# Down projection of the channel mix in split fp16, between the shared expert's products, and one write of zeros behind the experts' ends

## Chip, core and metric

The kernel runs on one core of a Trainium2 chip. The metric is the device time of one launch in microseconds (us). The engines are TensorE (PE, its weight loads PEld), VectorE (DVE), ScalarE (ACT), GpSimd (POOL) and SyncE (SP), which only issues DMAs. Each runs its own instruction queue in order; semaphores join them.

## Reference

`x` is 4096 tokens of 256 channels. With `LN` a layer norm without scale:

```
x = x + LN(rwkv(LN(x)))          # a time mix, then a channel mix
x = x + LN(moe(LN(x)))           # a shared expert and one of 8 routed experts per token
```

The channel mix in `rwkv`, on the result x2 of the time mix (`shift` moves by one token, ln2 with scale and offset):

```
xn2 = ln2(x2);  xk2, xr2 = two mixes of xn2 and shift(xn2)
kf  = square(relu(xk2 @ Wk_ffn.T))         # 1024 wide
kv  = kf @ Wv_ffn.T                        # the down projection, 1024 -> 256
x3  = x2 + sigmoid(xr2 @ Wr_ffn.T) * kv
```

The time mix is a recurrence over tokens (running maximum, numerator, denominator). Each expert is `gelu(x @ W1) * (x @ W2) @ W3`, width 1024; the routed one is the argmax of `x @ Wg`.

## The kernel before

**Stages.** The 4096 tokens are 16 chunks (NC) of 256 tokens. A software pipeline walks over steps i = -1 to 17 (`chunk_steps`; the middle steps run in a hardware loop, two steps to a turn). In step i the time mix works on chunk c0 = i, the channel mix on c1 = i-1, the shared expert and the choice of the routed expert on c2 = i-2, the end of the shared expert and the scatter of the tokens into rows by expert on c3 = i-3. Behind the steps come 39 slots of 128 rows for the routed experts (`slot_steps`).

**Split operands.** Most products run in fp16 with each operand split in a high and a low half: hi = fp16(v), by ScalarE, and lo = fp16(v - hi), by GpSimd or VectorE. `three` (L378 to L382) issues hi*hi, hi*lo and lo*hi into one sum. Weights are split once: `pieces` lists them, SP loads a piece (`load_own`), ScalarE writes its high half (`own_hi`), VectorE its low half (`own_lo`); OWN_LOADS, OWN_HI and OWN_LO say in which step. The down projection (L586, L589), the output projection of the time mix (L602) and the transposes (L389) are fp32. Its weights `w_fv` come by one DMA.

**Down projection.** For the four quarters q of 1024 hidden channels: TensorE `channel_mix_up(q)` into an `up` bank; ScalarE `relu_up(q)` (L796) into `relu_k[q % 2]` and `square(q)` (L804) into `kf`; TensorE `channel_mix_down(q)` takes the quarter's two tiles for the first 128 tokens, and with q = 3 all eight tiles for the other 128.

**Order of the queues.** Written out by hand, one list per engine and step. The names that the rest uses:

- TensorE: projection(0), (1), transposes of normed2 (`transpose_normed2`, L389), ranks, projection(2), `shared_down` of c3, transposes of xf, gate, `shared_gate`/`shared_up` 0 and 1, receptance, `channel_mix_up(0)`, `(1)`, transposes of the next chunk (`transpose_next`, L389), `channel_mix_up(2)`, `(3)`, then as in the code printed below.
- ScalarE: `xnT_norm` (L709) writes the next chunk's normalized, transposed input xnT from these transposes; `mix_hi(m)` (L831) the high halves of the mixes; `ln2` (L715) normed2.
- VectorE: `halo` (L1039, the column of xnT before its first token), `den_r` (L1116), `num` (L1131), `mix0` (L1049, the mixes for k, v and r from xnT and delta), `divide` (L1121), `rw` (L1136), mix0 for r, `x3_gate`, `x3_sum`, `x2_sum`, moments.
- GpSimd: delta2, inverse(0) (ten small operations for a norm), `now`, delta (L1549, xnT minus its shift), `mix_lo(0)`, `mix_lo(1)` (L1602), `sh_lo(0)` (L1596), scatter of c3 (two indirect DMAs, L1637), `sh_lo(1)`, `mix_lo(2)`, inverse(2), an offset (L1541), inverse(1) (its last operation is L1518), which `ln2` needs, `sh_lo(2)`, inverse(3), `sh_lo(3)`.

**Zeros.** The tokens of an expert end anywhere in a slot; the rows behind them must hold zeros. In step 16 (NC), ahead of the stores of the last split expert weights, SP writes zeros and a mark behind the tokens so far, 5 x 128 rows per expert, columns ID and up (`zeros_behind_tokens`, L304); GpSimd's scatter of the last chunks waits for these. In step 17 it writes 128 rows of the lower columns at each expert's end (`zeros_at_ends`, L313), then issues the first slots' loads (`first_slots`).

## Time and profile before

| | |
|---|---|
| three runs | 1004.53, 1005.79, 1005.34 us, median 1005.34 |
| profiled execution | 1005.74 us, its span 1004.0 us |
| busy TensorE, VectorE, ScalarE, GpSimd | 928.7, 722.7, 585.7, 587.6 us |
| DMA over the span | 156 GB/s |
| chunk steps, then slots | to about 670 us, then to 1004 us |

Times in the rows are microseconds from the start of the span. Busy time is the union of an engine's instructions, without the time in which its queue waits; a matmul's row shows its way through the pipeline, so starts, not ends, tell the pace of TensorE. "PEclk" is the clock granted to TensorE as a share of 2.4 GHz. What stands in brackets behind an instruction is how long its engine idled before it, and what released it.

### The profile page before, as it was taken

The page shows a single profiled execution, that of the slowest core. Times are in us where ns is not written, and L with a number is a line of the kernel's source. Part 1 is how long each engine was busy: PE and PEld are TensorE (multiplying, and loading weights), DVE is VectorE, ACT ScalarE, POOL GpSimd, SP SyncE. Part 2 cuts the span into 40 slices and gives each one's busy share as a digit, 9 for nine tenths or more (in the row PEclk, how much of TensorE's full clock was granted, in tenths as well). Part 3 has the DMA queues.
Part 4 walks back from the last instruction along what each step waited for, and adds up shares of the span by engine and source line. Part 5 has one row for each costly group of instructions (what it writes and reads, how often), then busy time and mean ns, then how long its engine had stood idle before and what let it go on. Part 6 is the DMA issues. An engine that isn't in the chain of part 4 may idle for free.

```text
span 1004.0 us, 28041 instructions
## 1 busy us (share of the span) xinstructions
PE 928.7 (93%) x9734; PEld 838.7 (84%) x9734; DVE 722.7 (72%) x1653; ACT 585.7 (58%) x1014; POOL 587.6 (59%) x800
## 2 busy tenths in 40 slices
PE   3377999999999999999999999699999999999994
PEld 2266888888888888888888888589999999999994
DVE  6888999999999999999999984444444444444442
ACT  4485778877878878868868855233333333333330
POOL 5446567667767867866866540454555555555553
PEclk9697999999999999999999999799999999999998
DMA  7212242351351252252152259845787788576510
GB/s 239 65 54 68 90 178 63 120 191 50 120 212 50 96 209 67 80 209 98 48 210 95 86 191 317 283 171 172 253 271 235 236 261 270 163 256 207 167 57 22
DMA packets 87339, 156.37 MB, mean 156 GB/s; under 512 B 5549, under 2 KB 68142, under 8 KB 82160
## 3 DMA queue, kind: packets, MB, share of 16 engines
q1 hardware_dynamic: 40352, 78.25, 22.9%
q10 hardware_dynamic: 42368, 60.38, 18.7%
q0 software_dynamic: 4560, 16.98, 4.4%
q8 instruction: 34, 0.56, 0.2%
q14 instruction: 25, 0.20, 0.1%
HBM read 183.59 MB, written 50.51 MB: 233 GB/s over the span
## 4 chain that ended last, share of the span: by engine, by line
PE 65%; DVE 9%; issue 9%; POOL 7%; ACTq 4%; ACT 3%; DMA 1%; POOLq 0%; DVEq 0%
PE up L380 13%; PE up L382 12%; PE up L381 12%; PE yp L380 6%; PE yp L382 6%; PE yp L381 6%; PE yp L586 2%; PE yp L589 2%; PE yp L602 2%; ACTq L933 2%; PE tp L389 2%; DVE arena L1020 1%; POOL mix_s L1602 1%; DVE er L1121 1%; POOL routed_rows L1637 1%
## 5 line engine op out<-in xcount | busy, mean ns | idle before, releaser
L380 PE MATMUL up<-mix_s,arena 128*128 128x128 f16 x1248 | 211.1, 219 | 0.4 <-DVE ex L1468 0.3
L381 PE MATMUL up<-mix_s,arena 128*128 128x128 f16 x1248 | 211.0, 219 | 0.0
L382 PE MATMUL up<-mix_s,arena 128*128 128x128 f16 x1248 | 211.0, 219 | 0.0
L380 PE MATMUL up<-xf_s,arena 128*128 128x256 f16 x512 | 140.7, 275 | 1.9 <-issue 1.9
L381 PE MATMUL up<-xf_s,arena 128*128 128x256 f16 x512 | 140.8, 275 | 0.0
L382 PE MATMUL up<-xf_s,arena 128*128 128x256 f16 x512 | 140.7, 275 | 0.0
L1700 POOL TENSOR_TENSOR kf_s<-ex,kf_s 128x512 f16<-128x512 f32 x78 | 90.2, 1156 | 84.1 <-ACT kf_s L979 84.0
L1468 DVE SCALAR_TENSOR_TENSOR ex<-up,ex 128x512 f32<-128x512 f32 x78 | 53.9, 692 | 102.1 <-ACT ex L973 101.9
L380 PEld LDWEIGHTS up<-mix_s,arena 128*128 128x128 f16 x1248 | 122.1, 98 | 1.3 <-DVE ex L1468 1.1
L381 PEld LDWEIGHTS up<-mix_s,arena 128*128 128x128 f16 x1248 | 122.1, 98 | 0.4
L382 PEld LDWEIGHTS up<-mix_s,arena 128*128 128x128 f16 x1248 | 122.1, 98 | 0.0
L973 ACT ACTIVATE ex<-up 128x512 f32<-128x512 f32 x78 | 45.9, 589 | 106.3 <-issue 57.2
L1596 POOL TENSOR_TENSOR sh_s<-gu,sh_s 128x512 f16<-128x512 f32 x64 | 76.1, 1190 | 43.0 <-ACT sh_s L824 42.7
L979 ACT ACTIVATE kf_s<-ex 128x512 f16<-128x512 f32 x78 | 49.1, 630 | 79.0 <-DVE ex L1468 67.3
L380 PE MATMUL yp<-arena,kf_s 128*128 128x256 f16 x312 | 85.0, 273 | 0.7 <-issue 0.7
L382 PE MATMUL yp<-arena,kf_s 128*128 128x256 f16 x312 | 85.0, 273 | 0.0
L381 PE MATMUL yp<-arena,kf_s 128*128 128x256 f16 x312 | 85.0, 273 | 0.0
L380 PE MATMUL yp<-arena,sh_s 128*128 128x256 f16 x256 | 71.2, 278 | 12.4 <-POOL sh_s L1596 12.4
L1602 POOL TENSOR_TENSOR mix_s<-mixed,mix_s 128x512 f16<-128x512 f32 x48 | 57.9, 1221 | 42.3 <-ACT mix_s L831 42.3
L381 PE MATMUL yp<-arena,sh_s 128*128 128x256 f16 x256 | 71.2, 278 | 0.0
L382 PE MATMUL yp<-arena,sh_s 128*128 128x256 f16 x256 | 71.1, 278 | 0.0
L380 PE MATMUL up<-mix_s,w_fk 128*128 128x256 f16 x256 | 70.1, 274 | 0.0
(228 smaller groups left out, 2864.8 us busy)
## 6 DMA issues: line engine op xcount, KB each, us to landing
arena<-w_split ACTq DMA_DIRECT2D x113, 1024.0 KB
arena<-in_W SPq DMA_DIRECT2D x24, 1024.0 KB, 6.6
w_split<-arena SPq DMA_DIRECT2D x24, 1024.0 KB, 9.3
rows<-routed_rows ACTq DMA_DIRECT2D x39, 261.0 KB, 3.0
arena<-w_split SPq DMA_DIRECT2D x9, 1024.0 KB
routed_rows<-x_in SPq DMA_DIRECT2D x8, 650.0 KB, 6.3
normed<-routed_rows ACTq DMA_DIRECT2D x37, 128.0 KB, 2.4
x_in<-in_x SPq DMA_DIRECT2D x16, 256.0 KB, 2.8
```

The costliest lines, as they stand in the source:

```text
L380: pe.matmul(out, stat(0), mov(0), start=first, stop=False)
L381: pe.matmul(out, stat(0), mov(1), start=False, stop=False)
L382: return pe.matmul(out, stat(1), mov(0), start=False, stop=last)
L389: m = pe.transpose(bank[:, k, t * P:(t + 1) * P], src[:, t, k * P:(k + 1) * P], ident[:])
L586: pe.matmul(yp[1][:, 0, :], kf[:, f, 0:P], w_fv[:, f, :], start=(f == 0), stop=(f == FT - 1))
L589: m = pe.matmul(yp[1][:, 1, :], kf[:, f, P:CH], w_fv[:, f, :], start=(f == 0), stop=(f == FT - 1))
L973: act.activation(slot_g[q], up[2 * q][:].rearrange("p k n -> p (k n)"), ACT.Gelu, scale=1 / WS).then_inc(S("slot_gelu"), 1)
L979: act.activation(slot_h[b][:, 0, q * FT // 2:(q + 1) * FT // 2, :], slot_g[q].rearrange("p (f n) -> p f n", n=P), ACT.Copy).then_inc(S("sl ...
L1468: dve.scalar_tensor_tensor(out=slot_g[q], in0=up[2 * q + 1][:].rearrange("p k n -> p (k n)"), scalar=HS / WS, in1=slot_g[q], op0=ALU.mult, ...
L1596: pool.tensor_tensor(sh_s[:, 1, 2 * g:2 * g + 2, :], gu[g % GUS][:], sh_s[:, 0, 2 * g:2 * g + 2, :], ALU.subtract).then_inc(S("sh_lo"), 1)
L1602: pool.tensor_tensor(mix_s[m][:, 1], mixed[m][:], mix_s[m][:, 0], ALU.subtract).then_inc(S("mix_lo"), 1)
L1700: pool.tensor_tensor(hs[:, 1], slot_g[q].rearrange("p (f n) -> p f n", n=P), hs[:, 0], ALU.subtract).then_inc(S("slot_h_lo"), 1)
```

## The change

- `w_fv` becomes a split piece (number 7, in buffer 2), loaded and split like the others. `kf` is kept as split halves in `kf_s`: `square(q)` stays in `relu_k`, ScalarE copies the high half (`kf_hi`), GpSimd subtracts for the low half (`kf_lo`), and `channel_mix_down` uses `three` in place of the fp32 product. The factor WS moves out of `x3_sum`.
- TensorE's order behind `channel_mix_up(3)`: `shared_gate(2)`, down 0 and 1, `shared_up(2)`, down 2 and 3, `output`.
- ScalarE's and GpSimd's lists get the new operations; `delta_of` stands between `kf_lo(1)` and `kf_lo(2)`.
- The zeros behind the tokens go. Zeros are written once, in step 17, whole rows, 128 at each expert's end, and the first slots wait for them; the scatter and the slots' later loads no longer do.
- In step 16 `sh_lo(1)` goes ahead of the scatter; in step 17 VectorE's `shared(2)` goes ahead of `last_slots`.

```diff
--- before.py
+++ after.py
@@ -67,7 +67,7 @@
         w_fk = sb("w_fk", [2, CT, F], F16)
-        w_fv = sb("w_fv", [FT, C])
+        w_fv = sb("w_fv", [2, FT, C], F16)
         w_gate = sb("w_gate", [2, CT, E], F16)
@@ -120,11 +120,9 @@
         relu_k = [sb(f"relu_k{b}", chan) for b in range(2)]
-        zero_row = x_in.rearrange("p t d -> p (t d)")[:, 0:ROW - ID]
-        zero_rest = ex.rearrange("p n k c -> p (n k c)")[:, 2 * CT * CH:2 * CT * CH + ID]
+        zero_row = ex.rearrange("p n k c -> p (n k c)")[:, 2 * CT * CH:2 * CT * CH + ROW]
         mixed2 = relu_k
         kf_s = sb("kf_s", [2, FT, CH], F16)
-        kf = kf_s.rearrange("p h f n -> p (h f n)").bitcast(F32).rearrange("p (f n) -> p f n", f=FT)
         sh_s = sb("sh_s", [2, FT, CH], F16)
@@ -150,7 +148,6 @@
         expert_int = sb("expert_int", [2, E], I32)
-        zero_at = sb("zero_at", [E], I32)
         end_at = sb("end_at", [E], I32)
@@ -192,14 +189,16 @@
             pieces.append((tiles(a[n]), (CT, CT, FT)[m], (F, F, C)[m], shared_w[:, m]))
+        pieces.insert(7, (tiles(a["fvT"]), FT, C, flat(w_fv)))
         N_OWN = len(pieces)
-        NEEDS_KVR, NEEDS_FFN, NEEDS_SHARED = 3, 6, 8
-        OWN_HI = {(-2, 0): (0, 3), (-1, 2): (3, 4), (0, 0): (4, 6), (0, 2): (6, 7), (1, 1): (7, 9)}
-        OWN_LO = {(-2, 0): (0, 3), (-1, 1): (3, 4), (0, 1): (4, 6), (1, 3): (6, 7), (2, 3): (7, 8), (2, 0): (8, 9)}
-        OWN_LOADS = {(-1, 0): (4, 6), (0, 0): (6, 7), (0, 1): (8, 9), (1, 1): (7, 8)}
-        OWN_BUFFER = [0, 1, 2, 4, 0, 1, 3, 1, 4]
+        NEEDS_KVR, NEEDS_FFN, NEEDS_FV, NEEDS_SHARED = 3, 6, 8, 9
+        OWN_HI = {(-2, 0): (0, 3), (-1, 2): (3, 4), (0, 0): (4, 6), (0, 2): (6, 8), (1, 1): (8, 10)}
+        OWN_LO = {(-2, 0): (0, 3), (-1, 1): (3, 4), (0, 1): (4, 6), (1, 3): (6, 7), (1, 0): (7, 8), (2, 3): (8, 9),
+                  (2, 0): (9, 10)}
+        OWN_LOADS = {(-1, 0): (4, 6), (0, 0): (6, 8), (0, 1): (9, 10), (1, 1): (8, 9)}
+        OWN_BUFFER = [0, 1, 2, 4, 0, 1, 3, 2, 1, 4]
         own_raw = raw + [c.rearrange("p h n -> p (h n)").bitcast(F32) for c in cut]
@@ -292,25 +291,14 @@
             load_own(3)
-            sp.dma_start(w_fv[:], tiles(a["fvT"])).then_inc(S("fv_in"), 16)
-            def zeros_behind_tokens():
-                sp.wait_ge(S("zero_at"), 1)
+            def zeros_at_ends():
+                sp.wait_ge(S("end_at"), 1)
                 sp.wait_ge(S("zero_row"), 1)
-                n = 2 * CH // P + 1
-                for e in range(E):
-                    at = sp.value_load(zero_at[0:1, e:e + 1], min_val=0, max_val=E * REGION - n * P)
-                    sp.dma_start(routed_rows[bass.ds(at, n * P), ID:].rearrange("(n p) d -> p n d", p=P),
-                                 zero_row.unsqueeze(1).broadcast_to([P, n, ROW - ID])).then_inc(S("zeroed"), 16)
-            def zeros_at_ends():
-                sp.wait_ge(S("end_at"), 1)
-                sp.wait_ge(S("zero_rest"), 1)
                 for e in range(E):
                     at = sp.value_load(end_at[0:1, e:e + 1], min_val=0, max_val=E * REGION - P)
-                    sp.dma_start(routed_rows[bass.ds(at, P), 0:ID], zero_rest).then_inc(S("zeroed_rest"), 16)
+                    sp.dma_start(routed_rows[bass.ds(at, P)], zero_row).then_inc(S("zeroed"), 16)
@@ -337,6 +325,7 @@
                 sp.wait_ge(S("scattered_xf"), 16 * TT)
+                sp.wait_ge(S("zeroed"), 16 * E)
                 for b in range(2):
@@ -360,8 +349,6 @@
                     load_expert(e, m)
-                if at_step(i, NC):
-                    zeros_behind_tokens()
                 for e, m in early_piece(i, p, h) + last_late(i, p, h) + late_now(i, p, h):
@@ -371,8 +358,6 @@
-            sp.wait_ge(S("zeroed"), 16 * E)
-            sp.wait_ge(S("zeroed_rest"), 16 * E)
@@ -578,16 +563,17 @@
                     if at_step(i, 1) and q == 0:
-                        pe.wait_ge(S("fv_in"), 16)
+                        pe.wait_ge(S("piece_lo"), NEEDS_FV)
                     if q == 0:
                         wait(pe, S("y_sh"), c1 - 1)
-                    wait(pe, S("kf"), 4 * c1 + q + 1)
+                    wait(pe, S("kf_lo"), 4 * c1 + q + 1)
                     for f in (2 * q, 2 * q + 1):
-                        pe.matmul(yp[1][:, 0, :], kf[:, f, 0:P], w_fv[:, f, :], start=(f == 0), stop=(f == FT - 1))
+                        three(pe, yp[1][:, 0, :], lambda s: kf_s[:, s, f, 0:P], lambda s: w_fv[:, s, f, :],
+                              f == 0, f == FT - 1)
                     if q == 3:
                         for f in range(FT):
-                            m = pe.matmul(yp[1][:, 1, :], kf[:, f, P:CH], w_fv[:, f, :], start=(f == 0),
-                                          stop=(f == FT - 1))
+                            m = three(pe, yp[1][:, 1, :], lambda s: kf_s[:, s, f, P:CH], lambda s: w_fv[:, s, f, :],
+                                      f == 0, f == FT - 1)
                         m.then_inc(S("fv_mm"), 1)
@@ -654,11 +640,13 @@
                     ranks(c2)
-                for q in range(4):
-                    channel_mix_down(q)
                 shared_gate(2)
+                channel_mix_down(0)
+                channel_mix_down(1)
+                shared_up(2)
+                channel_mix_down(2)
+                channel_mix_down(3)
                 output()
-                shared_up(2)
                 shared_gate(3)
@@ -792,7 +780,7 @@
                         wait(act, S("fk_mm"), n + 1)
-                        wait(act, S("kf"), n - 1)
+                        wait(act, S("kf_lo"), n - 1)
                         act.activation(relu_k[q % 2][:], up[(11 + q) % 4][:], ACT.Relu,
@@ -800,8 +788,14 @@
                         wait(act, S("relu"), n + 1)
+                        act.activation(relu_k[q % 2][:], relu_k[q % 2][:], ACT.Square).then_inc(S("kf"), 1)
+                def kf_hi(q):
+                    if on(c1):
+                        wait(act, S("kf"), 4 * c1 + q + 1)
                         wait(act, S("fv_mm"), c1)
-                        act.activation(kf[:, 2 * q:2 * q + 2, :], relu_k[q % 2][:], ACT.Square).then_inc(S("kf"), 1)
+                        act.activation(kf_s[:, 0, 2 * q:2 * q + 2, :], relu_k[q % 2][:],
+                                       ACT.Copy).then_inc(S("kf_hi"), 1)
@@ -891,12 +885,16 @@
                 relu_up(1)
+                kf_hi(0)
+                square(1)
                 xnT_norm()
-                square(1)
+                kf_hi(1)
                 relu_up(2)
+                square(2)
+                kf_hi(2)
                 relu_up(3)
-                square(2)
                 square(3)
+                kf_hi(3)
                 sigmoid()
@@ -981,7 +979,6 @@
                         act.wait_ge(S("scattered_rest"), 16 * TT * 2)
-                        act.wait_ge(S("zeroed_rest"), 16 * E)
                     at = rows_of(j)
@@ -1053,7 +1050,7 @@
                 wait(dve, S("delta2"), c + 1)
-                wait(dve, S("kf"), 4 * c)
+                wait(dve, S("kf_lo"), 4 * c)
                 for m in (1, 0):
@@ -1156,7 +1153,7 @@
                 wait(dve, S("x3a"), c + 1)
-                dve.scalar_tensor_tensor(out=gate_r[:], in0=gate_r[:], scalar=0.5 * WS, in1=x2[:],
+                dve.scalar_tensor_tensor(out=gate_r[:], in0=gate_r[:], scalar=0.5, in1=x2[:],
                                          op0=ALU.mult, op1=ALU.add).then_inc(S("x3"), 1)
@@ -1278,8 +1275,6 @@
                     placing(c3, 1 - p, h + p - 2)
-                if at_step(i, NC):
-                    zeros_after()
                 if on(c1):
@@ -1299,6 +1294,7 @@
                     places_of_slots()
+                    shared(2)
                     last_slots()
@@ -1348,7 +1344,8 @@
                     x2_moments(c0)
-                shared(2)
+                if not at_step(i, NC + 1):
+                    shared(2)
                 if at_step(i, NC):
@@ -1364,15 +1361,8 @@
                     dve.wait_ge(S("denominator"), 4 * NC)
-                    dve.memset(zero_rest, 0.0).then_inc(S("zero_rest"), 1)
+                    dve.memset(zero_row, 0.0).then_inc(S("zero_row"), 1)
                 own(2)
-            def zeros_after():
-                dve.wait_ge(S("normed"), TT * NC)
-                dve.memset(zero_row, 0.0).then_inc(S("zero_row"), 1)
-                dve.wait_ge(S("next_row"), NC - 2)
-                dve.tensor_copy(zero_at[:], next_row[:, 0, :]).then_inc(S("zero_at"), 1)
@@ -1596,6 +1586,12 @@
+                def kf_lo(q):
+                    if on(c1):
+                        wait(pool, S("kf_hi"), 4 * c1 + q + 1)
+                        pool.tensor_tensor(kf_s[:, 1, 2 * q:2 * q + 2, :], relu_k[q % 2][:],
+                                           kf_s[:, 0, 2 * q:2 * q + 2, :], ALU.subtract).then_inc(S("kf_lo"), 1)
@@ -1627,8 +1623,6 @@
                     if on(c) and not at_step(i, NC + 1):
-                        if at_step(c, NC - 2):
-                            pool.wait_ge(S("zeroed"), 16 * E)
                         wait(pool, S("placed"), c + 1)
@@ -1655,13 +1649,20 @@
                 now_of()
+                kf_lo(0)
+                kf_lo(1)
                 delta_of()
+                kf_lo(2)
+                kf_lo(3)
                 scatter_expert_input()
...
                 sh_lo(0)
+                if at_step(i, NC):
+                    sh_lo(1)
                 scatter(c3, 1 - p)
-                sh_lo(1)
+                if not at_step(i, NC):
+                    sh_lo(1)
                 mix_lo(2)
```

## Rows read from the trace of the kernel before

**Rows 1.** Stretch, us, busy (x) of PE, PEld, DVE, ACT, POOL; PEclk, DMA, GB/s
```profile
110.00:600.00 490.00, 487.41 (x4111) 431.55 (x4109) 456.51 (x1017) 384.64 (x659) 339.33 (x447) 1.00 0.34 121
```

**Rows 2.** Groups by line and shape: count, busy us, mean ns, idle before
```profile
L979 ACT ACTIVATE kf_s<-ex 128x512 f16<-128x512 f32 x78 | 49.1, 630 | 79.0 <-DVE ex L1468 67.3 <-PE yp L382 10.4 <-PE up L382 1.4
...
L1014 DVE SCALAR_TENSOR_TENSOR w_fk<-arena,w_fk 128x2048 f16<-128x2048 f32 x1 | 2.3, 2284 | 0.0
...
L1700 POOL TENSOR_TENSOR kf_s<-ex,kf_s 128x512 f16<-128x512 f32 x78 | 90.2, 1156 | 84.1 <-ACT kf_s L979 84.0
```

**Rows 3.** Timeline of TensorE: start us, us, instruction, [idle before it <- releaser]
```profile
121.44 0.60 PE L389 MATMUL tp<-ident,normed 128*128 128x128 f32 x4
...
306.19 0.65 PE L389 MATMUL tp<-ident,normed 128*128 128x128 f32 x4 [0.17 <-ACT normed L715]
...
323.32 0.60 PE L389 MATMUL tp<-ident,normed 128*128 128x128 f32 x4
...
326.37 3.62 PE L586 MATMUL yp<-w_fv,kf_s 128*128 128x256 f32 x16
...
333.28 0.27 PE L380 MATMUL up<-xf_s,arena 128*128 128x256 f16 x1
...
334.59 1.89 PE L602 MATMUL yp<-w_o,val 128*128 128x256 f32 x8
...
342.87 0.60 PE L389 MATMUL tp<-ident,normed 128*128 128x128 f32 x4
...
600.53 0.66 PE L389 MATMUL tp<-ident,normed 128*128 128x128 f32 x4 [1.08 <-ACT normed L715]
```

**Rows 4.** Timeline of ScalarE in the step from 306 to 343 us
```profile
323.26 0.63 ACT L804 ACTIVATE kf_s<-relu_k 128x512 f32<-128x512 f32 x1
...
324.25 1.04 ACT L709 ACTIVATE xnT<-tp,vec 128x256 f32<-128x256 f32 x2
...
341.68 1.07 ACT L715 ACTIVATE normed<-x,inv 128x256 f32<-128x256 f32 x2
```

**Rows 5.** Timeline of GpSimd in the same step
```profile
309.28 1.04 POOL L1549 TENSOR_TENSOR delta<-xn2T 128x512 f32<-128x512 f32 x1 [0.90 <-DVE xn2T L1039]
...
325.65 1.43 POOL L1549 TENSOR_TENSOR delta<-xnT 128x512 f32<-128x512 f32 x1 [4.37 <-DVE xnT L1039]
329.29 2.28 POOL L1602 TENSOR_TENSOR mix_s<-mixed,mix_s 128x512 f16<-128x512 f32 x2 [2.21 <-ACT mix_s L831]
...
341.32 0.20 POOL L1518 TENSOR_TENSOR inv<-inv 128x2 f32<-128x2 f32 x1
```

**Rows 6.** Timeline of VectorE in the same step
```profile
325.32 0.17 DVE L1039 COPY xnT<-xnT 128x2 f32<-128x2 f32 x1 [0.67 <-ACT xnT L709]
...
326.10 1.53 DVE L1131 TENSOR_TENSOR val<-mixed,dist 128x512 f32<-128x512 f32 x1
327.55 1.66 DVE L1049 SCALAR_TENSOR_TENSOR mixed<-delta,vec,xnT 128x256 f32<-128x256 f32 x4
...
332.51 0.72 DVE L1136 TENSOR_TENSOR val<-val,er 128x512 f32<-128x512 f32 x1
```

**Rows 7.** Timelines of VectorE and GpSimd in the next step
```profile
363.39 0.16 DVE L1039 COPY xnT<-xnT 128x2 f32<-128x2 f32 x1
...
367.13 2.27 POOL L1602 TENSOR_TENSOR mix_s<-mixed,mix_s 128x512 f16<-128x512 f32 x2 [2.08 <-ACT mix_s L831]
```

**Rows 8.** Busy time in one stretch behind the middle, columns as in rows 1
```profile
600.00:610.00 10.00, 8.38 (x76) 7.00 (x77) 8.15 (x17) 6.03 (x11) 4.01 (x7) 0.83 0.86 287
```

**Rows 9.** Timelines of SP's queue, GpSimd and TensorE behind the last chunk
```profile
604.39 12.96 SPq L304 DMA_DIRECT2D routed_rows<-x_in  x8
...
641.84 0.20 POOL L1541 TENSOR_TENSOR rows<-mv,inv 128x2 f32<-128x2 f32 x1 [5.75 <-DMA routed_rows<-rows,row_of]
...
643.39 0.40 PE L380 MATMUL yp<-arena,sh_s 128*128 128x256 f16 x1 [7.36 <-POOL sh_s L1596]
...
654.08 9.26 SPq L313 DMA_DIRECT2D routed_rows<-ex  x8
```

More of the change, by code:

```diff
@@ L294, in _ @@
             load_own(3)
-            sp.dma_start(w_fv[:], tiles(a["fvT"])).then_inc(S("fv_in"), 16)
-            def zeros_behind_tokens():
-                sp.wait_ge(S("zero_at"), 1)
-                sp.wait_ge(S("zero_row"), 1)
-                n = 2 * CH // P + 1
-                for e in range(E):
-                    at = sp.value_load(zero_at[0:1, e:e + 1], min_val=0, max_val=E * REGION - n * P)
-                    sp.dma_start(routed_rows[bass.ds(at, n * P), ID:].rearrange("(n p) d -> p n d", p=P),
-                                 zero_row.unsqueeze(1).broadcast_to([P, n, ROW - ID])).then_inc(S("zeroed"), 16)
             def zeros_at_ends():
                 sp.wait_ge(S("end_at"), 1)
-                sp.wait_ge(S("zero_rest"), 1)
+                sp.wait_ge(S("zero_row"), 1)
                 for e in range(E):
                     at = sp.value_load(end_at[0:1, e:e + 1], min_val=0, max_val=E * REGION - P)
-                    sp.dma_start(routed_rows[bass.ds(at, P), 0:ID], zero_rest).then_inc(S("zeroed_rest"), 16)
+                    sp.dma_start(routed_rows[bass.ds(at, P)], zero_row).then_inc(S("zeroed"), 16)
             def half(w, part):
```

## Prediction

> **What bounds the kernel now.** I read the busy time of the long middle stretch first, then the timeline of each engine over one chunk step, then the stretch behind the last chunk. In the middle TensorE is busy 487.4 of 490 us at a granted clock of 1.00 [rows 1]. That looks like a kernel bound by TensorE alone, in which every microsecond of products taken away comes back. The timelines correct this. The transposes of normed2 mark a step: thirteen steps between the first and the last of these rows take (600.53 - 121.44)/13 = 36.85 us each [rows 3]. ScalarE's normalization that these transposes need runs from 341.68 to 342.75, and they start at 342.87 [rows 3, 4]: they start the moment it lands. In the step before, TensorE idled 0.17 us there for the same instruction [rows 3]. So there is a second limit of the same length as TensorE's work. Follow it back: the normalization waits for GpSimd's inverse(1), which ends at 341.52; GpSimd has worked in an unbroken row up to it since mix_lo(0) at 329.29, 12.2 us earlier [rows 5]; mix_lo(0) comes behind VectorE's mix0, at 327.55, which waited for GpSimd's delta (325.65 to 327.08), and that for the halo column at 325.32 [rows 5, 6]. The halo comes from the transposes at 323.32. Between 306.19 and 323.32 TensorE works without a gap, on nothing that the change touches [rows 3]. This is a ring: transposes of normed2, 17.1 us of products, transposes of the next chunk, GpSimd's queue, transposes of normed2. The down projection (326.37 to 333.28) lies beside the ring.
>
> **TensorE's saving.** The 32 products of the down projection, fp32 now, take 333.28 - 326.37 = 6.91 us by 16 products (two records each). A split product of the same 256 columns costs (334.59 - 333.28)/12 = 0.109 us [rows 3], so 16 x 3 of them take 5.24 us. That is 1.67 us a step less, 27 us over 16 chunks, if TensorE's work set the time. That a split product is dearer than this is excluded by the same row.
>
> **ScalarE.** Four copies kf_hi per chunk, 0.63 us each [rows 2], 0.5 us apart where they don't wait for the instruction before them (square(0) at 323.26, one other, then the normalization at 324.25 [rows 4]). kf_hi(0) takes the place of the normalization of xnT, and with square(1) ahead of it too that moves 1.0 us, to 325.25 to 326.3. kf_hi(1) ends at 326.9. relu(2), square(2), kf_hi(2), relu(3), square(3), kf_hi(3) each wait for the one before, in good part: kf_hi(2) ends near 328.75 and kf_hi(3) near 330.6. ScalarE has room for these.
>
> **GpSimd.** Four subtractions kf_lo, 1.156 us each by the row of the same form [rows 2], 4.6 us a step, in the middle of the ring. It idled 4.37 us before delta [rows 5], and kf_lo(0), from 325.0 to 326.15, hides there. kf_lo(1) can't start before 326.95, and delta now stands behind it; kf_lo(2) and kf_lo(3) stand between delta and mix_lo(0). What is queued behind these is everything down to inverse(1), so the whole unbroken row of 12.2 us moves with mix_lo(0).
>
> How much? The halo is at 326.35. VectorE and GpSimd get in each other's way on operations that read two operands from SBUF: delta took 1.43 us while VectorE worked on such operations and 1.04 in another place of the step [rows 5], and VectorE's num took 1.53 us beside it while the equally large rw took 0.72 [rows 6]. I take that over. kf_lo(1) is held until about 327.15 by den_r and ends at 328.3; num waits for that and ends at 328.85; delta goes to 329.75; kf_lo(2), which has been ready, goes first and ends at 330.9, while VectorE's four mix0 (1.66 us [rows 6]) wait. Then these and kf_lo(3) share 2.55 us, in either order (if kf_lo(3) is first, mix_hi(0) is late; if mix0 is first, kf_lo(3) is), so mix_lo(0) starts at 333.45 and not at 329.29: +4.15 us. In every other step VectorE reaches the halo late by its own queue (363.39, mix_lo(0) at 367.13 [rows 7]), later than the moved xnT: there kf_lo(1) ends at 365.15, delta at 366.6, kf_lo(2) at 367.8, mix_lo(0) starts at 370.35: +3.2 us. The mean is 3.7 us a step.
>
> The lower bound leaves out the blocking: 1.04 for delta, kf_lo(3) right behind kf_hi(3), mix_lo(0) at 331.75 and 368.3, which is +2.4 and +1.2, mean 1.8. I take 3.7, since both rows show the blocking at just this place.
>
> The Trainium skill, "SBUF - State Buffer", section on who interferes with whom, says that a VectorE instruction with two SBUF inputs and a GpSimd instruction that reads SBUF exclude each other for a whole instruction. By that rule the step grows 3.7 us, without it 1.8; the trace agrees (1.53 us against 0.72).
>
> **On TensorE beside the ring.** down(2) waits until 331.0 for kf_lo(2), down(3) until some 333.5 for kf_lo(3), output then for rw, whose reciprocal starts 3 us later than before. The output ends near 339 instead of 336.3; gate(3), up(3) and two projections (5.24 us) bring TensorE to 344.3, and the normed2 transposes come at 342.87 + 4.15 = 347.0. So TensorE idles 2 to 3 us there and some 2.5 us earlier, 5.5 us a step, and the 1.67 us saved is part of that idle time. The moved shared_up(2) covers the wait for down(2), and can't cover more.
>
> **The ring's steps.** There are 15 intervals between transposes of normed2 with a down projection in them (the 13 above and the two before 121.44). 15 x 3.7 = 55 us.
>
> **The clock.** Between 600 and 610 us two idle stretches of about 1.1 us (the first is in [rows 3]) are followed by a mean granted clock of 0.83 [rows 8]: 10 x (1 - 0.83) = 1.7 us of work lost at 1.2 GHz instead of 2.4. Whether 2 to 3 us of idle before the transposes do that in each step is open: between nothing and 15 x 1.7 = 26 us. I take one step in four, 7 us.
>
> **The beginning.** The down weights become a split piece: one more VectorE pass of 2.28 us [rows 2] in a step where VectorE is busy, and one on ScalarE: between 0 and 4 us, I take 2.
>
> **The end.** The zeros behind the tokens occupy SP's queue for 12.96 us ahead of the last stores [rows 9]; without them the last expert piece, x3_gate and with it the scatter come 2 to 3 us earlier, and so does the landing for which GpSimd waited 5.75 us and TensorE then 7.36 us [rows 9]. The landing itself stays. shared(2) ahead of last_slots gives up to 1 us. Against that, the zeros at the ends (9.26 us of SP queue from 654.08 [rows 9]) are rows 1.5 times as long and must now have landed before the first slots are read: between 0 and 4 us, I take 1.5. Together -2, between -8 and +3.
>
> **Sum** against the profiled execution's own 1005.74 us (span 1004.0): + 55 + 7 + 2 - 2 = 1067.7. The median is 0.4 us lower: 1067.
>
> **Rivals.** Less than 0.2% (2 us) can't be told from no change here.
> 1. The ring grows as above, with the clock falling in a few steps: 1050 to 1080 us. Chance 0.50.
> 2. The blocking between VectorE and GpSimd is lighter: 15 x 1.8 = 27 us and the small terms, 1033; with half of it 1047. For it: which engine wins is not shown by a row. 1025 to 1050: 0.23.
> 3. The clock falls in every step: 1005.3 + 55 + 26 = 1086. For it: TensorE now idles 5.5 us a step. Against it: the row shows it behind two stretches in close succession only [rows 8]. Above 1080: 0.15.
> 4. Faster. The tight fit of normalization and transposes is a result of TensorE's pace and GpSimd's idle 4.37 us in front of delta takes up the four subtractions: then 27 us go, with the end 29, to 976. It decides if mix_lo(0) starts no later after the transposes of the next chunk than the 5.97 us of now (329.29 - 323.32). Against it: kf_lo(1) can't start before 326.95. Chance 0.08.
> 5. Both effects meet near nothing (a shift of some 0 to 1 us): 0.04.
>
> The range that leaves out no more than 2 in 10 reaches from 1033 (rival 2's bound) to 1090. Faster 0.08, same 0.03, slower 0.89.
>
> **What the changed kernel's profile would show.** The transposes of normed2 about 40.5 us apart, with idle time on TensorE in front of them put down to ScalarE's normalization; TensorE's busy share in the middle near 87%; GpSimd's delta some 3 us later behind the transposes of the next chunk and mix_lo(0) 9 to 10 us behind them instead of 6 to 7; num and mix0 stretched; down(2) and down(3) waiting for GpSimd. If mix_lo(0) is late but the transposes are not, the ring is drawn wrong; if they are 35 us apart, rival 4 holds; half clock behind each idle stretch is rival 3.

## The result and the profile after

Slower: 1052.31 us median (1049.34 to 1054.52, 4 runs) against 1004.98 us (4 runs), a ratio of 1.0469, 95% interval 1.0453 to 1.0485. The profiled execution took 1049.34 us, its span 1047.5 us: 43.5 us more than the span of before. Of all runs told here one was slow and is left out, 5311 us for the kernel before with fewer products and the scatters early.

Where the 43.5 us are is read from the marks of the steps. First the timeline of TensorE in the kernel after; the transposes of normed2 (L374; those at 344.40 are of the next chunk) answer to [rows 3]:

```profile
126.13 0.38 PE L374 MATMUL tp<-ident,normed 128*128 128x128 f32 x2
...
344.40 0.60 PE L374 MATMUL tp<-ident,normed 128*128 128x128 f32 x4
...
353.23 0.28 PE L365 MATMUL yp<-w_fv,kf_s 128*128 128x256 f16 x1 [0.46 <-POOL kf_s L1592]
...
358.33 0.48 PE L588 MATMUL yp<-w_o,val 128*128 128x256 f32 x1 [1.65 <-DVE val L1133]
...
366.98 0.33 PE L374 MATMUL tp<-ident,normed 128*128 128x128 f32 x1 [0.16 <-ACT normed L703]
...
643.16 0.44 PE L374 MATMUL tp<-ident,normed 128*128 128x128 f32 x2 [2.28 <-ACT normed L703]
```

Thirteen steps take (643.16 - 126.13)/13 = 39.77 us each, 2.92 more than before. From the first transposes of normed2 (48.88 us here, 49.79 before) to the last, the 15 steps take 594.28 us against 550.74: all 43.5 us. What lies ahead is 0.9 us shorter, what lies behind 0.9 longer. From the transposes of the next chunk to those of normed2 the step shown takes 22.58 us against 19.55, the following one (384.10 to 407.16) 23.06 against 20.04 (359.94 to 379.98): +3.0 each. The other part, 344.40 - 327.27 = 17.13 us, is what it was.

The middle stretch in the kernel after (windows, columns as in [rows 1]), and its longest waits (engine, line, released by: us in total, times, longest):

```profile
110.00:640.00 530.00, 475.64 (x4321) 411.59 (x4322) 490.83 (x1011) 420.04 (x712) 399.20 (x496) 1.00 0.32 111
```

```profile
PE yp L588 <- DVE val L1133: 22.3, 13, 2.6
PE yp L365 <- POOL kf_s L1592: 15.0, 27, 1.3
PE up L365 <- DVE gu L1241: 14.2, 13, 1.2
...
PE tp L374 <- ACT normed L703: 2.9, 9, 1.2
```

TensorE is 90% busy at a granted clock of 1.00, not 99%. Its idle time, 54 us or 4.1 us a step, lies ahead of the output projection, the down projection and the first projection, not ahead of the transposes.

VectorE, GpSimd and ScalarE in the step of 344.40 (timelines of the kernel after), to be held against [rows 4 to 6]:

```profile
347.44 0.17 DVE L1036 COPY xnT<-xnT 128x2 f32<-128x2 f32 x1 [1.71 <-ACT xnT L697]
...
348.22 1.65 DVE L1128 TENSOR_TENSOR val<-mixed,dist 128x512 f32<-128x512 f32 x1
350.88 3.37 DVE L1046 SCALAR_TENSOR_TENSOR mixed<-delta,vec,xnT 128x256 f32<-128x256 f32 x4 [1.01 <-POOL delta L1539]
354.17 3.34 DVE L1118 RECIPROCAL er<-er 128x512 f32<-128x512 f32 x1
357.55 0.73 DVE L1133 TENSOR_TENSOR val<-val,er 128x512 f32<-128x512 f32 x1
...
360.61 0.48 DVE L1140 SCALAR_TENSOR_TENSOR x<-normed,spread,yp 128x256 f32<-128x256 f32 x1
...
363.20 0.15 DVE L1026 BATCH_NORM_AGGREGATE mv<-stats 128x2 f32<-128x6 f32 x1
```

```profile
348.00 1.32 POOL L1592 TENSOR_TENSOR kf_s<-relu_k,kf_s 128x512 f16<-128x512 f32 x1 [0.79 <-ACT kf_s L797]
349.28 1.49 POOL L1539 TENSOR_TENSOR delta<-xnT 128x512 f32<-128x512 f32 x1
350.73 2.44 POOL L1592 TENSOR_TENSOR kf_s<-relu_k,kf_s 128x512 f16<-128x512 f32 x2
354.20 1.15 POOL L1598 TENSOR_TENSOR mix_s<-mixed,mix_s 128x512 f16<-128x512 f32 x1 [1.02 <-ACT mix_s L825]
...
364.04 0.44 POOL L1498 TENSOR_TENSOR inv<-mv,eps_ws 128x2 f32<-128x2 f32 x1
...
365.61 0.20 POOL L1508 TENSOR_TENSOR inv<-inv 128x2 f32<-128x2 f32 x1
```

```profile
346.37 1.03 ACT L697 ACTIVATE xnT<-tp,vec 128x256 f32<-128x256 f32 x2
```

Counted from the transposes of the next chunk (t0): xnT starts at t0 + 1.97 (before 0.93), the halo at 3.04 (before 2.00), mix0 at 6.48 (before 4.23), mix_lo(0) at 9.80 (before 5.97), rw at 13.15 (before 9.19), x2_sum at 16.21 (before 13.20), the end of inverse(1) at 21.41 (before 18.20). So the four mix0 take 3.37 us beside GpSimd's subtractions instead of 1.66 [rows 6], and VectorE's row has moved by 1.0 us at the halo and by 3.0 at x2_sum, about as GpSimd's has at inverse(1) (3.2).

Which row ends last can be read where they meet. GpSimd works from mix_lo(0) to inverse(1) without a wait for another engine. The moments of x2 are ready at 363.35, 0.7 us before inverse(1) begins (364.04); in the step of 384.10 it is the same 0.7. The moments of x3 are ready 0.3 us before inverse(2), in both. So GpSimd's row ends last, and VectorE's is only 0.3 us shorter.

### The profile page after: what moved, and what is told of

It reads as the page before. It is cut to its first block, busy times and chain, and to the rows that moved or that the text cites. A ratio compares the mean times of both kernels' runs of the same rounds, so it can differ in the third digit from the quotient of the medians.

```text
span 1047.5 us, 28645 instructions
## 1 busy us (share of the span) xinstructions
PE 911.9 (87%) x9990; PEld 813.7 (78%) x9990; DVE 763.0 (73%) x1652; ACT 629.1 (60%) x1079; POOL 661.9 (63%) x864
## 4 chain that ended last, share of the span: by engine, by line
PE 27%; DVE 17%; issue 16%; POOL 15%; ACTq 13%; ACT 6%; DMA 3%; SPq 1%; POOLq 0%; DVEq 0%
ACTq L931 6%; PE up L365 5%; PE up L367 5%; PE up L366 5%; PE yp L365 3%; PE yp L366 3%; PE yp L367 3%; ACTq L954 3%; DVE mixed L1046 2%; POOL kf_s L1592 2%; DVE er L1118 2%; ACTq L934 2%; POOL mix_s L1598 2%; POOL routed_rows L1631 2%; DMA routed_rows<-rows,row_of 2%
## 5 line engine op out<-in xcount | busy, mean ns | idle before, releaser
L1592 POOL TENSOR_TENSOR kf_s<-relu_k,kf_s 128x512 f16<-128x512 f32 x64 | 83.6, 1314 | 95.7 <-ACT kf_s L797 95.7
L365 PE MATMUL yp<-w_fv,kf_s 128*128 128x256 f16 x256 | 70.9, 277 | 18.8 <-POOL kf_s L1592 18.8
L365 PE MATMUL yp<-arena,sh_s 128*128 128x256 f16 x256 | 71.2, 278 | 12.5 <-POOL sh_s L1586 12.5
L1046 DVE SCALAR_TENSOR_TENSOR mixed<-delta,vec,xnT 128x256 f32<-128x256 f32 x96 | 65.8, 737 | 9.3 <-POOL delta L1539 9.3
```

The source lines that it names most:

```text
L365: pe.matmul(out, stat(0), mov(0), start=first, stop=False)
L1046: dve.scalar_tensor_tensor(out=mixed[m][:, k, :], in0=delta[:, k, :], scalar=vec[:, MK + m, k:k + 1], in1=x[:, k, 0:CH], op0=ALU.mult, op1 ...
L1592: pool.tensor_tensor(kf_s[:, 1, 2 * q:2 * q + 2, :], relu_k[q % 2][:], kf_s[:, 0, 2 * q:2 * q + 2, :], ALU.subtract).then_inc(S("kf_lo"), 1)
```

## The experiments

"The kernel before" and "the kernel after" are the two of the change; each edit is to one of them.

**Is TensorE's saving worth anything?** The kernel before with fewer products, and with only the edits of the zeros and of the end.

```diff
-                        for f in range(FT):
+                        for f in range(FT // 2):
```

> The kernel before, with 4 of the 8 fp32 products of the down projection's second 128 tokens left out: 4 x 0.43 = 1.73 us less for TensorE a chunk, as much as the change saves it, and nothing else touched. Ring theory (the queue of GpSimd sets the step, TensorE only keeps pace): 1003 to 1005 us, the transposes of normed2 still 36.8 us apart, idle time of 1.7 us a step on TensorE in front of them. Rival (TensorE sets the time): 16 x 1.73 = 28 us less, 977.

Measured 1004.11 us against 1005.12, ratio 0.9992 (0.9981 to 1.0003), a step of 36.84 us against 36.91. 1.73 us a step less on TensorE are worth nothing. Rival 4 fell here: something of the same length as TensorE's work holds the step. In this trace it is GpSimd's row: 12.29 us from mix_lo(0) to inverse(1) in the step of t0 = 324.40, without a wait for another engine; meanwhile the moments of x3 on VectorE are ready 1.1 us before inverse(2) begins.

> The kernel before, with the change's zeros alone: one write behind the ends, no zeros behind the tokens, sh_lo(1) ahead of the scatter in step 16, shared(2) ahead of the last slot table in step 17. As predicted for the end: 2 to 4 us less, 1002. Rival (the first slots wait for the landing of the zeros, the scatter's landing is as late as before): 0 to 2 us more, 1006.

Measured 1005.36 us, ratio 1.001 (0.9998 to 1.0021): the rewritten zeros, the moved sh_lo(1) and shared(2) are worth nothing either way. The 2 to 4 us that I expected did not come.

**Which part costs what?** The kernel after with the low halves' subtraction cut to 8 columns of one tile (first diff), then the high halves' copy too (second), what is no longer written being zeroed once at the start; and the kernel before with the new order of TensorE alone, still with fp32 products.

```diff
-    pool.tensor_tensor(kf_s[:, 1, 2 * q:2 * q + 2, :], relu_k[q % 2][:],
-                       kf_s[:, 0, 2 * q:2 * q + 2, :], ALU.subtract)
+    pool.tensor_tensor(kf_s[:, 1, 2 * q:2 * q + 1, 0:8], relu_k[q % 2][:, 0:1, 0:8],
+                       kf_s[:, 0, 2 * q:2 * q + 1, 0:8], ALU.subtract)
```

> The changed kernel, with GpSimd's kf_lo cut to 8 columns of one tile (the low half stays zero elsewhere); waits, ScalarE's copies and the split products all stay. Ring theory: the four subtractions on GpSimd and their blocking are the whole loss; what stays is xnT one microsecond late in every other step: 36.8 to 37.4 us a step, 1005 to 1014 us. Rival (the dependent copies on ScalarE, or TensorE's waits for the halves, cost it): most of the 47 us stay, 1035 or more.

```diff
-    act.activation(kf_s[:, 0, 2 * q:2 * q + 2, :], relu_k[q % 2][:], ACT.Copy)
+    act.activation(kf_s[:, 0, 2 * q:2 * q + 1, 0:8], relu_k[q % 2][:, 0:1, 0:8], ACT.Copy)
```

> The changed kernel with both kf_lo on GpSimd and kf_hi on ScalarE cut to 8 columns of one tile (the halves stay zero elsewhere). TensorE's new order and its 1.67 us fewer a step stay, with next to no cost on the other engines. Theory as mended by e2 and e3 (the serial copies on ScalarE and the subtractions on GpSimd are the cost; the order costs only where the down projection ends late): the ring is as before, and TensorE's saving is worth nothing: 1003 to 1012 us. Rival 1 (the order alone costs 31 us in the changed kernel too): 1030 or more. Rival 2 (TensorE's saving shows once the halves are free): 980.

```diff
-    for q in range(4):
-        channel_mix_down(q)
     shared_gate(2)
+    channel_mix_down(0)
+    channel_mix_down(1)
+    shared_up(2)
+    channel_mix_down(2)
+    channel_mix_down(3)
     output()
-    shared_up(2)
```

> The kernel before, fp32 products as they were, with TensorE's order of the change alone (shared_gate(2), down 0 and 1, shared_up(2), down 2 and 3, output). Output comes 1.31 us later, and its way over x2 to GpSimd's inverse(1) had 0.55 us to spare: 0.7 us a step, 15 steps, 1010 to 1018 us. Rival (the order is free since the products are the same): 1005.

Measured: 1035.19 us without most of the subtraction (1.0306, 1.0284 to 1.0328), 1009.75 us without most of either (1.0047, 1.0029 to 1.0065), 1036.61 us for the order alone (1.0318, 1.0296 to 1.034). The first and the last missed what I expected.

With both halves cut, 4.5 us of the 47 are left. Giving ScalarE its full copies back costs 25.4 us more, giving GpSimd its subtractions 17.1 more, in this order; the subtractions without the copies were not run. I had priced ScalarE's copies at nothing but the moved xnT. VectorE and ScalarE in the step of t0 = 334.40, the kernel after with the small low halves:

```profile
337.44 0.17 DVE L1036 COPY xnT<-xnT 128x2 f32<-128x2 f32 x1 [1.70 <-ACT xnT L697]
...
339.92 1.67 DVE L1046 SCALAR_TENSOR_TENSOR mixed<-delta,vec,xnT 128x256 f32<-128x256 f32 x4 [1.01 <-POOL delta L1539]
...
344.89 1.66 DVE L1133 TENSOR_TENSOR val<-val,er 128x512 f32<-128x512 f32 x1
```

```profile
340.92 0.63 ACT L797 ACTIVATE kf_s<-relu_k 128x512 f16<-128x512 f32 x1
341.45 0.58 ACT L805 ACTIVATE gate_r<-yp 128x512 f32<-128x512 f32 x1
341.93 0.62 ACT L825 ACTIVATE mix_s<-mixed 128x512 f16<-128x512 f32 x1
```

The mixes take 1.67 us again, so it is GpSimd's subtractions that stretch them to 3.37. But the halo is still 3.04 us behind the transposes, and mix_hi(0) (L825), queued behind the last copy and the sigmoid, starts only at t0 + 7.5. GpSimd's mix_lo(0) then comes at t0 + 8.2 in both kinds of steps (before 5.97 and 7.19: 1.6 us later in the mean, and the step is 38.67 us, 1.8 longer), and its row runs on past the reciprocal: rw takes 1.66 us and not 0.73. So GpSimd's 4.6 us of subtractions are not the cause alone.

The order alone costs 31 us because the fp32 down projection, now behind gate(2) and up(2), ends later. VectorE and GpSimd in that kernel:

```profile
348.90 0.69 DVE L1156 SCALAR_TENSOR_TENSOR gate_r<-gate_r,yp 128x512 f32<-128x512 f32 x1 [2.09 <-PE yp L589]
...
351.55 0.87 DVE L1145 SCALAR_TENSOR_TENSOR x<-normed,spread,yp 128x256 f32<-128x256 f32 x2
```

```profile
353.45 0.20 POOL L1510 TENSOR_TENSOR inv<-mv,eps_ws 128x2 f32<-128x2 f32 x1 [2.60 <-DVE mv L1031]
```

x3_gate waits 2.09 us for the down projection, x3_sum behind it takes 1.78 us beside GpSimd instead of 0.69, x2_sum stands behind both in VectorE's queue, and GpSimd's inverses wait 2.60 us for VectorE. A second way to the same end: through VectorE, not through GpSimd's row.

**Is TensorE's old order better with split operands?** The kernel after with the order of before.

> The changed kernel with TensorE's old order (down 0 to 3, shared_gate(2), output, shared_up(2)). If the order costs here what it costs in e3: 31 us less, 1021. By the traces, the down projection now ends when kf_lo(3) has come, whatever the order, and TensorE waits for rw afterwards: 1040 to 1052 us.

Measured 1057.41 us (1.0522, 1.0503 to 1.054), 5 us worse than the change and above both cases that I had named. The products wait for the low halves anyway (45.3 us in the stretch from 110 to 640 us, 15.0 with the new order, whose gate(2) and up(2) fill that wait), so the 31 us that the order costs on fp32 products aren't there to be saved. The two costs don't add.

What the 5 us are, the trace tells in part, by the clock. Two of the eleven steps from 143 to 571 us keep a granted clock of 1.00 between the transposes of the next chunk and those of normed2, and take 22.25 and 22.56 us there, as in the kernel after (22.26 and 22.59). In the other nine the mean is below that, 0.93 in eight. In the step of t0 = 345.78 the clock falls to its lower level, 1.2 GHz, behind waits of 1.10, 1.73 and 0.47 us for the low halves (windows, columns as in [rows 1]):

```profile
356.00:358.00 2.00, 2.00 (x11) 1.40 (x10) 2.00 (x1) 2.00 (x4) 2.00 (x3) 0.50 0.00 0
```

The split products come 0.64 us apart by threes there and 0.33 elsewhere, x2_sum waits 0.95 us for the output, and the step's part is 23.37 us long. The same three waits stand in the step of t0 = 427.13, which keeps its clock.

**Is GpSimd's row the limit?** The scatters moved out of the middle of the row to behind `now`, in both kernels, and ScalarE's `y_shared` ahead of `ln0` so that they can start (in the kernel before together with the fewer products).

```diff
                 now_of()
+                scatter(c3, 1 - p)
...
                 sh_lo(0)
-                scatter(c3, 1 - p)
                 sh_lo(1)
```

> The changed kernel, with the two scatters of GpSimd moved from between sh_lo(0) and sh_lo(1) into its idle time ahead of kf_lo(0), and y_shared on ScalarE ahead of ln0 so that they can start. Nothing of the change is touched. Ring theory: GpSimd's unbroken row between mix_lo(0) and inverse(1) is 3.0 us shorter; the other way into inverse(1), from rw over output, x2 and its moments, has 0.7 us to spare, so 0.7 to 1.5 us a step come back: 1030 to 1042 us. If GpSimd's row were the only limit: 45 us back, 1007. Rival (TensorE's waits for the halves set the step): 1052.

> The kernel before with both: 1.73 us of TensorE's products a step left out, as in e1, and the scatters moved into GpSimd's idle time, as in e6. Two limits of the same length: either alone gives nothing (e1 gave 1 us), both together give what TensorE was spared, less what the way over output and x2 allows: 980 to 990 us. Rival (a third limit stands right behind): 1000 or more.

Measured 1058.18 us (1.0529, 1.0496 to 1.0561) and 1007.95 us (1.0016, 1.0001 to 1.003). Both missed: with some 2.5 us taken out of its row the step got no shorter but 0.8 to 0.9 us longer, 40.94 us for 40.04 over twelve steps in the first and 37.67 for 36.84 (fewer products alone) in the second. VectorE and GpSimd, the kernel after with the scatters early:

```profile
360.89 3.34 DVE L1118 RECIPROCAL er<-er 128x512 f32<-128x512 f32 x1
364.26 1.70 DVE L1133 TENSOR_TENSOR val<-val,er 128x512 f32<-128x512 f32 x1
```

```profile
360.91 2.28 POOL L1598 TENSOR_TENSOR mix_s<-mixed,mix_s 128x512 f16<-128x512 f32 x2 [1.02 <-ACT mix_s L825]
363.15 2.27 POOL L1586 TENSOR_TENSOR sh_s<-gu,sh_s 128x512 f16<-128x512 f32 x2
```

Now sh_lo(1) lies where the scatters were, and rw takes 1.70 us beside it. In the kernel before with fewer products and these edits GpSimd waits 1.03 us for the moments of x3 ahead of inverse(2). In the step of t0 = 329.97 they are ready at t0 + 15.0, as in the kernel before; with fewer products alone they are ready at t0 + 14.1. The 0.9 us between are rw and the mixes for r, which take 0.89 + 1.77 us beside GpSimd's sh_lo instead of 0.72 + 0.86. So VectorE's row is a third one of nearly the same length, and the edit itself made it longer. What a shorter row of GpSimd is worth with VectorE's left as it is, these runs don't show.

The clock adds to it. In four of the eleven steps from 138 to 537 us its mean is 0.92 between the two transposes; in the one of t0 = 440.99 it falls behind TensorE's wait for rw, to 0.50 from 454 to 456 us:

```profile
453.27 3.40 PE L602 MATMUL yp<-w_o,val 128*128 128x256 f32 x8 [2.57 <-DVE val L1136]
```

In the step of t0 = 366.40 the same output, behind a wait of 2.82 us at a clock of 1.00, takes 1.99 us.

**Can VectorE's row be shortened?** Three orders of the kernel after: ScalarE's xnT_norm ahead of kf_hi(0) and square(1), GpSimd's delta_of ahead of all four kf_lo, and both.

```diff
+                xnT_norm()
                 kf_hi(0)
                 square(1)
-                xnT_norm()
```

```diff
+                delta_of()
                 kf_lo(0)
                 kf_lo(1)
-                delta_of()
```

> The kernel after, with two instructions back in the places that they had before: ScalarE norms the next chunk (xnT) right behind the second relu, ahead of the first copy and the second square, and GpSimd writes delta ahead of all four subtractions of the relu's low halves. Nothing is added or left out. My theory now: what a step grew by (2.9 us) is VectorE's unbroken row from the halo to the moments of x2, whose start waits for xnT (1.03 us later than before), whose first products wait for delta (1.0 us) and run slowly beside GpSimd's subtractions (1.7 us). The first two come back, the third stays: a step of 37.8 to 38.8 us, 1020 to 1036 us in all. Rival: GpSimd's own row (mix_lo to the inverse of the moments), with 3.8 us of new work ahead of it, sets the step whatever VectorE does: no change, 1048 to 1055. Second rival: the subtractions now all lie on the products of mix0, which lose more than before: 1036 to 1048.

> The kernel after with only ScalarE's norm of the next chunk moved ahead (right behind the second relu). My theory: the halo copy starts 1 us earlier, but delta on GpSimd still stands behind two subtractions, which then wait for ScalarE's copies that come 1.1 us later: most of the gain is lost, 1042 to 1054. Rival: the halo is what is late, and the whole 1 us comes back a step: 1035 to 1040.

> The kernel after with only GpSimd's delta moved ahead of the four subtractions. My theory: the wait of mix0 for delta (1.0 us a step) goes, the products still start behind the later halo and run beside all four subtractions: 0.5 to 1 us a step, 1036 to 1046. Rival: GpSimd waits for xnT with the subtractions queued behind it, so that mix_lo(0) comes as late as now and nothing comes back: 1048 to 1055.

Measured: both 1071.09 us (1.0665, 1.0641 to 1.0688), xnT alone 1053.89 (1.0496, 1.047 to 1.0522), delta alone 1077.5 (1.0733, 1.0705 to 1.0761). The second is as expected: the halo comes at t0 + 2.0, but mix0 still at t0 + 6.6, since delta stands behind two subtractions (347.76 and 352.32 with t0 = 345.75). The two with delta ahead are 19 and 25 us worse than the change, outside every case that I had named. GpSimd and VectorE with both moved, t0 = 355.34:

```profile
357.67 1.43 POOL L1539 TENSOR_TENSOR delta<-xnT 128x512 f32<-128x512 f32 x1 [5.06 <-DVE xnT L1036]
359.07 2.90 POOL L1592 TENSOR_TENSOR kf_s<-relu_k,kf_s 128x512 f16<-128x512 f32 x2
...
364.56 1.15 POOL L1592 TENSOR_TENSOR kf_s<-relu_k,kf_s 128x512 f16<-128x512 f32 x1 [0.51 <-ACT kf_s L797]
365.68 2.73 POOL L1598 TENSOR_TENSOR mix_s<-mixed,mix_s 128x512 f16<-128x512 f32 x2
368.36 1.34 POOL L1586 TENSOR_TENSOR sh_s<-gu,sh_s 128x512 f16<-128x512 f32 x1
```

```profile
359.57 3.46 DVE L1046 SCALAR_TENSOR_TENSOR mixed<-delta,vec,xnT 128x256 f32<-128x256 f32 x4
362.96 3.34 DVE L1118 RECIPROCAL er<-er 128x512 f32<-128x512 f32 x1
366.33 1.05 DVE L1133 TENSOR_TENSOR val<-val,er 128x512 f32<-128x512 f32 x1
367.31 2.67 DVE L1046 SCALAR_TENSOR_TENSOR mixed<-delta,vec,xnT 128x256 f32<-128x256 f32 x2
...
371.52 0.87 DVE L1140 SCALAR_TENSOR_TENSOR x<-normed,spread,yp 128x256 f32<-128x256 f32 x2
```

VectorE's mixes do start 2.25 us earlier behind t0 (4.23 instead of 6.48) and rw 2.16 us earlier (10.99). All of it is lost by x2_sum (16.18 instead of 16.21). GpSimd's delta waits 5.06 us for the halo with kf_lo(0) queued behind it; the next relu waits for kf_lo(0), so the last kf_lo ends at t0 + 10.4, the last part of the down projection starts then, and mix_lo(0) comes at t0 + 10.3 (9.80 in the kernel after). The row behind it has slipped off the reciprocal: rw and the mixes for r, 1.05 + 2.67 us, run until GpSimd's sh_lo(0) ends at 369.7. In the kernel after they took 0.73 + 0.87. GpSimd's own row ends later too, inverse(1) at t0 + 22.5 instead of 21.4, and twelve steps from 130.67 to 627.53 take 41.4 us each (40.0 in the kernel after).

**All three rows lighter at once,** on the kernel before: fewer products, scatters early, and

```diff
-                dve.reciprocal(er[:], er[:])
+                dve.reciprocal(er[:, 0:1], er[:, 0:1])
```

> The kernel before with all three rows made shorter at once: TensorE leaves out half of the down projection's products for the second half of a chunk (1.73 us a step), GpSimd's scatters stand ahead of delta, and VectorE takes the reciprocal of only one of the two column blocks (1.67 us a step less, in the row from halo to the moments of x2). Products and half of the reciprocals are left out, so the output isn't the reference's. My theory, three rows of nearly equal length that all end in the same inverse: the first two alone gave nothing, with the third some 1.5 us a step come back, 979 to 990 us. Rival: yet another wait holds the step at its length (ScalarE's chain from the squares to ln2): 998 to 1008.

Measured 993.94 us against 1005.55, ratio 0.9892 (0.9873 to 0.9912): 1.1% less, where two rows alone gave nothing, but 11.6 us and not 15 to 26, between the two cases that I had named. And the gain isn't in the steps. The first and last of twelve full ones on TensorE, in this kernel:

```profile
116.86 0.38 PE L389 MATMUL tp<-ident,normed 128*128 128x128 f32 x2
...
558.71 0.33 PE L389 MATMUL tp<-ident,normed 128*128 128x128 f32 x1
```

(558.71 - 116.86)/12 = 36.82 us a step. The kernel before has (564.40 - 121.44)/12 = 36.91. Of the 13.0 us between the two spans (1004.0 and 991.0), 1.1 came in these twelve, 4.6 ahead of them, 1.7 in the last step and 5.6 behind it. Why, inside the steps, shows beside the reciprocal (VectorE, then GpSimd; the step of t0 = 318.68):

```profile
324.33 1.74 DVE L1121 RECIPROCAL er<-er 128x256 f32<-128x256 f32 x1
326.10 1.37 DVE L1136 TENSOR_TENSOR val<-val,er 128x512 f32<-128x512 f32 x1
327.39 2.68 DVE L1049 SCALAR_TENSOR_TENSOR mixed<-delta,vec,xnT 128x256 f32<-128x256 f32 x2
```

```profile
324.65 2.27 POOL L1602 TENSOR_TENSOR mix_s<-mixed,mix_s 128x512 f16<-128x512 f32 x2 [2.38 <-ACT mix_s L831]
326.88 2.90 POOL L1596 TENSOR_TENSOR sh_s<-gu,sh_s 128x512 f16<-128x512 f32 x2
```

The reciprocal is 1.60 us shorter, and the two groups behind it take 1.37 + 2.68 = 4.05 us instead of 0.72 + 0.87 = 1.59. In the kernel before the reciprocal (3.34 us from 329.14) covers GpSimd's mix_lo(0), mix_lo(1) and all but 0.2 us of sh_lo(0), and the scatters, beside which nothing is stretched, lie beside rw and the mixes for r. So VectorE's row is hardly shorter: the moments of x3 are ready at t0 + 14.8 instead of 15.0. What a step gains when all three rows are really shorter is not shown.

## Why the prediction was right, and where it was off

Right: the direction, the kind (rival 1's bounds, 1050 to 1080 us, hold the 1052.31), the row that ends last in the changed kernel (GpSimd's, by 0.3 us), and the reason that the products saved on TensorE are worth nothing. Too high by 15 us at the median and by 18 in the profiled execution (its terms give +62, measured +43.6), term by term:

- **The steps**, +55 us predicted, 43.5 measured in the profiled execution: 2.9 us a step for 3.7. The step "the whole unbroken row of 12.2 us moves with mix_lo(0)" was too simple. Its head moved as worked out: +3.83 and +3.0 us in the two kinds of steps (394.30 - 384.10 = 10.2, before 7.19) for +4.15 and +3.2. The transposes at its end moved by 3.03 and 3.02. In the first kind the row shrank from 12.23 us (329.29 to 341.52) to 11.61 (354.20 to 365.81): the stretch of the two scatters, from the end of sh_lo(0) to the next sh_lo, takes 2.9 us instead of 3.6.
- **The ring** was one of three, and I drew only one. GpSimd's row, VectorE's row from halo to moments, and TensorE's work are so close in length that 1.7 us less of the last, or 2.5 less of the first with it, bring nothing (the second in part because the moved work stretches VectorE's); and the change lengthens the first two alike: VectorE's by 1.04 us (xnT later on ScalarE), 1.2 (num stretched and the wait for delta) and 1.7 (mix0 stretched), of which rw shows 3.96 and x2_sum 3.0. That one row alone predicted nearly the right number is partly luck: had the change lengthened VectorE's row by 0.3 us more, that row would have set the step. One reading of the rows was wrong as well: mix0 at 327.55 did not wait for delta, done at 327.08, but followed num, which ended at 327.63.
- **Blocking.** 3.7 us with it and 1.8 without it; 2.9 was measured. That VectorE's two-input operations and GpSimd's stretch each other is shown by mix0, 1.67 us with the subtractions cut down and 3.37 with them, and by kf_lo, 1.31 us in the mean against 1.16 for the same subtraction in the slots. By the Trainium skill, "SBUF - State Buffer", on who interferes with whom, each excludes the other for a whole instruction; the traces agree: the stretched operations double, and the reciprocal, with a single input, takes 3.34 us beside GpSimd's rows as elsewhere.
- **The clock**, +7: nothing. The granted clock is 1.00 from 110 to 640 us, though TensorE idles 54 us there. The fall of rival 3 is real in other orders: from 110 to 600 us the mean is 0.96 with TensorE's old order and 0.98 with delta ahead. The sum of the idle time doesn't tell it: with the old order TensorE idles 43 us of these 490, in the kernel after 52. Nor do the waits just ahead of it, as the two pairs of steps above show. Why the kernel after keeps its clock no run shows.
- **The beginning**, +2: -0.9. **The end**, -2: +0.9; the run of these edits alone shows no gain. The first slot's load now starts behind the zeros, at 708.71 us, 65.6 us behind the last transposes of normed2 (64.1 before).
- **ScalarE.** The prediction said that it has room. It has room in busy time, but the copies put mix_hi(0) late by themselves: with small low halves they cost 25 us (1035.19 against 1009.75). In the kernel after mix_hi(0) waits for mix0 instead (1.46 us, at 353.49), so the copies' delay lies beside GpSimd's, and the sum didn't miss it.

TensorE's idle time was forecast at 5.5 us a step, in part ahead of the transposes; it is 4.1 us and came ahead of output (22.3 us for rw), of the down projection and of the first projection.

What is left open: how much a step would gain if GpSimd's row alone or all three rows became shorter without stretching each other; what decides whether the clock falls behind a wait; and whether an order exists that keeps GpSimd's subtractions under the reciprocal with the split products. Of the orders tried here that do the whole computation, none was faster than the kernel before.

## What to carry to other kernels

When TensorE is 99% busy and a second chain lands just in time, look for a third before pricing the change: take the queue of each engine from the step's mark to the join, and write down how late each may be. New work of two SBUF inputs on GpSimd costs VectorE time too (here 1.7 us of the mixes beside 2.4 us of subtractions), unless VectorE is at something that isn't slowed, here the reciprocal; where the work lies counts as much as how long it is. Taking work out of a row moves what stood behind it, and what that now lies beside has to be priced as well. And a cheaper operand format isn't cheaper if its preparation goes to the engines in the chain.

## What the hardware showed that I had not expected

The reciprocal of 128x512 took 3.34 us in every kernel, whatever GpSimd did beside it; the product rw of the same size took 0.71 to 1.70. Four 128x256 mixes took 1.66 us with GpSimd quiet and 3.37 to 3.46 beside its subtractions; two took 0.87, and 2.67 beside its low halves. Over the 16 chunks the mixes' group (groups by line, VectorE; the kernel after, then the one with both moves) shows it at once, where the kernel before has 41.3 us at a mean of 484 ns:

```profile
L1046 DVE SCALAR_TENSOR_TENSOR mixed<-delta,vec,xnT 128x256 f32<-128x256 f32 x96 | 65.8, 737 | 9.3 <-POOL delta L1539 9.3
```

```profile
L1046 DVE SCALAR_TENSOR_TENSOR mixed<-delta,vec,xnT 128x256 f32<-128x256 f32 x96 | 90.8, 998 | 2.2 <-POOL delta L1539 2.2
```
